# A four-layer graph network on one core: two single-head products in three rounded passes, one output slot, and another order of work in every queue

## What is computed

```
# x (128, 128, 512), adj (128, 128, 128); _ln = layer norm over the features
h = max(_ln(x), 0);  x = x + elu-attention, one head, values h           # layer 0
h = max(_ln(x), 0);  x = x + two GAT layers:                             # layer 1
      L1a: xl = h @ W1 (1024 columns, 4 heads), softmax over sources, elu
      L1b: xl2 = g @ W2 (512 columns, 1 head), softmax, out = attn^T @ xl2
h = max(_ln(x), 0);  x = x + attn(h) @ h, one head                       # layer 2
h = max(_ln(x), 0);  x = x + relu(attention, 8 heads of 64, h @ W_proj)  # layer 3
```

## Time and profile before

| | us |
|---|---|
| median of 3 runs | 3081.05 (3080.08 to 3081.91) |
| the profiled execution | 3083.84 |
| its span, first to last instruction | 3082.1 |
| TensorE busy | 2976.9 (97% of the span) |
| VectorE busy | 2480.0 (80%) |
| ScalarE busy | 2319.9 (75%) |
| GpSimd busy | 2263.2 (73%) |
| transfers: mean busy share of the 16 DMA engines | 35% |

### The profile page before, as it was taken

The page is one execution under the profiler, slowest core; times in us unless marked ns, Lnnn a source line. Parts: engine busy times, 40 slices in busy tenths (PEclk is TensorE's granted clock), DMA queues, the critical chain, the costliest instruction groups (busy, mean ns, idle before and its releaser), DMA issues. The chain is left out here.

```text
span 3082.1 us, 79166 instructions
## 1 busy us (share of the span) xinstructions
PE 2976.9 (97%) x21040; PEld 2746.1 (89%) x21040; DVE 2480.0 (80%) x8101; ACT 2319.9 (75%) x6433; POOL 2263.2 (73%) x3214
## 2 busy tenths in 40 slices
PE   7899999999999999999999999999999999999974
PEld 5789999999999999999999999999999999999964
DVE  3578888888888888888888888888888888888852
ACT  2567787778877788777787778877788777787752
POOL 3467777777777777777777777777777777777753
PEclk6999999999999999999999999999999999999985
DMA  5123333333333333333333333333333333333332
GB/s 195 34 69 123 117 119 122 108 124 118 119 123 106 125 117 119 122 109 122 118 119 121 108 122 120 120 118 112 121 120 119 118 110 122 120 120 119 96 107 93
DMA packets 205558, 355.71 MB, mean 115 GB/s; under 512 B 51904, under 2 KB 117568, under 8 KB 188736
## 3 DMA queue, kind: packets, MB, share of 16 engines
q1 hardware_dynamic: 205120, 350.66, 34.8%
HBM read 314.93 MB, written 35.59 MB: 114 GB/s over the span
## 5 line engine op out<-in xcount | busy, mean ns | idle before, releaser
L1454 POOL TENSOR_SCALAR rs<-mv,rs 128x1 f32<-128x1 f32 x512 | 357.6, 698 | 109.2 <-POOL rs L1451 108.8
L997 ACT ACTIVATE eT<-eT,tc 128x128 f32<-128x128 f32 x1024 | 314.1, 389 | 161.3 <-POOL eT L1534 161.3
L432 PE MATMUL bank_b<-w_hi,hT_hi 128*128 128x344 f32 x1536 | 419.8, 328 | 5.6 <-DVE g L1277 3.8
L432 PE MATMUL bank_c<-w_hi,g_hi 128*128 128x258 f32 x2048 | 414.1, 283 | 4.7 <-DVE x L1204 4.7
L432 PE MATMUL bank_c<-w_lo,g_hi 128*128 128x258 f32 x2048 | 414.5, 284 | 0.0
L432 PE MATMUL bank_b<-w_lo,hT_hi 128*128 128x344 f32 x1536 | 408.2, 320 | 0.0
L1329 DVE CUSTOM_DVE_ANT_0 t_all_L<-t_all_L,mask 128x128 f32<-128x128 f32 x1024 | 368.6, 413 | 27.0 <-DMA t_all_L<-t_dram_L 26.5
L432 PE MATMUL bank_b<-w_hi,hT_lo 128*128 128x344 f32 x1536 | 357.0, 327 | 0.0
L432 PE MATMUL bank_c<-w_hi,g_lo 128*128 128x258 f32 x2048 | 351.8, 284 | 0.0
L432 PE MATMUL bank_e<-w_hi,hT_hi 128*128 128x264 f32 x1024 | 341.1, 347 | 5.5 <-DVE out_sb L1372 5.4
L1540 POOL TENSOR_TENSOR eT<-eT,shift_all 128x512 f32<-128x512 f32 x256 | 331.1, 1294 | 4.6 <-ACT eT L997 4.4
(11 more groups left out here) (158 smaller groups left out, 8577.5 us busy)
## 6 DMA issues: line engine op xcount, KB each, us to landing
shift_all<-shift_dram SPq DMA_DIRECT2D x128, 1024.0 KB, 5.3
t_all_L<-t_dram_L SPq DMA_DIRECT2D x128, 512.0 KB, 3.7
x_in<-in_x SPq DMA_DIRECT2D x128, 256.0 KB, 2.6
t_all_L1a<-t_dram_L1a SPq DMA_DIRECT2D x128, 256.0 KB, 3.2
out<-out_sb SPq DMA_DIRECT2D x128, 256.0 KB, 3.1
t_all_L<-t_dram_L SPq DMA_DIRECT2D x256, 64.0 KB, 3.1
adj_in<-in_adj SPq DMA_DIRECT2D x128, 64.0 KB, 3.0
t_dram_L1a<-t_rows_L1a SPq DMA_DIRECT2D x512, 0.5 KB
```

Of the source, the lines that this page charges most:

```text
L432: last = mm(bank[:, 0:width], a[:, c * P:(c + 1) * P], w[:, c, b * width:(b + 1) * width], start=(first and c == chunks[0] and n == 0), st ...
L997: last = activation(eT[:, k, :], eT[:, k, :], ACT.Prelu, bias=tc3[:, k:k + 1], alpha=SLOPE)
L1454: ts(b, mv[layer][:, 0:1], r, -1.0, ALU.mult, ALU.mult).then_inc(sem(f"rs_made{layer}"), 1)
```

## The change

Two of the three single-head products, `product_L1b` and `product_L2`, are made like the projections, in three rounded passes (`product_of_parts`). They need four new parts each: the transposed probabilities are rounded as they leave PSUM (`pT_L1b`, `pT_L2`, now F32R), VectorE subtracts for their low part (`pT_lo_L1b`, `pT_lo_L2`), ScalarE rounds the values (`v_hi_L1b`, `v_hi_L2`), and VectorE (`v_lo_L1b`) or GpSimd (`v_lo_L2`) subtracts for theirs. The output tile has one slot where it had two, the probabilities are written over the scores (`p1 = e1`), and the scratch `product` has two rows where it had four, which makes `columns_L0` and `columns_L2` wait for each other. Two counters are folded into others (`bn_made` into `mv_made`, `ident_loaded` into `att_in`). The order of the calls is another one in all five queues, and where a step begins has moved: some calls that opened a step now close the one before, with the graph number one lower. On SyncE the small sends come ahead of the large spreads, and the store of the output and `spread_L2` close the step. SKEW is 11.

Left out below: the waits that only follow the renumbering.

```diff
-SKEW = 12
+SKEW = 11
...
-        XR, MR, LR, TR, X1R, X2R, X3R, OR = 3, 10, 8, 4, 3, 2, 4, 2
+        XR, MR, LR, TR, X1R, X2R, X3R, OR = 3, 10, 8, 4, 3, 2, 4, 1
...
-        product = sb("product", [P, 4, D], BF16)
+        product = sb("product", [P, 2, D], BF16)
...
-        p1 = {k: sb(f"p_{k}", [P, P]) for k in one}
-        pT1 = {k: sb(f"pT_{k}", [P, P]) for k in one}
+        p1 = e1
+        split = ("L1b", "L2")
+        pT1 = {k: sb(f"pT_{k}", [P, P], F32R if k in split else F32) for k in one}
+        pT1_lo = {k: sb(f"pT_lo_{k}", [P, P], F32R) for k in split}
+        v_hi = {k: sb(f"v_hi_{k}", [P, D], F32R) for k in split}
+        v_lo = {k: sb(f"v_lo_{k}", [P, D], F32R) for k in split}
...
-                dst = (x3[:, c, :] if c < 2 else out_sb[:, c - 2, :])
+                dst = (x3[:, c, :] if c < 2 else (out_sb[:, 0, :], xl2[:, 0:D])[c - 2])
...
                 load(t.graph(0))
-                store(t.graph(12))
-                spread_L2(t.graph(7))
                 send_L0(t.later_graph(2))
-                spread_L0(t.later_graph(2))
                 send_L1b(t.graph(5))
                 send_shift_L3(t.graph(10))
+                spread_L0(t.later_graph(2))
                 spread_L1b(t.graph(5))
                 spread_shift_L3(t.graph(10))
                 send_L1a(t.graph(3))
-                spread_L1a(t.graph(3))
                 send_L3(t.graph(9))
                 send_L2(t.graph(6))
+                spread_L1a(t.graph(3))
                 spread_L3(t.graph(9))
+                store(t.graph(11))
+                spread_L2(t.graph(6))
...
+            def product_of_parts(key, bank):
+                for n, (a, v) in enumerate(((pT1[key], v_hi[key]), (pT1[key], v_lo[key]), (pT1_lo[key], v_hi[key]))):
+                    last = mm(bank, a[:], v[:], start=(n == 0), stop=(n == 2))
+                last.then_inc(sem(f"{key}_out"), 1)
...
             def product_L2(t, g):
                 if g.live:
-                    pe.wait_ge(sem("L2_pT"), g.made())
-                    if t.full:
-                        pe.wait_ge(sem("L2_pT"), g.made())
...
+                        pe.wait_ge(sem("flat_copied"), g.made(2))
+                    product_of_parts("L2", bank_a[:])
...
             def product_L1b(t, g):
                 if g.live:
-                    pe.wait_ge(sem("L1b_pT"), g.made())
+                    pe.wait_ge(sem("L1b_pT_lo"), g.made())
+                    pe.wait_ge(sem("L1b_v_lo"), g.made())
...
-                    mm(bank_c[:, 1, :], pT1["L1b"][:], xl2[:, 0:D], start=True, stop=True).then_inc(sem("L1b_out"), 1)
+                    product_of_parts("L1b", bank_c[:, 1, :])
...
-                project_L1b_first_high(t, t.graph(5))
                 project_L1b_first_low(t, t.graph(5))
+                turn_h3(t, t.graph(9))
                 project_L1b_last(t, t.graph(5))
                 turn_mask(t, t.graph(3))
-                turn_h3(t, t.graph(9))
+                product_L3_last(t, t.graph(11))
                 turn_prob_L1a(t, t.graph(4))
-                product_L3_last(t, t.graph(11))
+                product_L3_first(t, t.graph(11))
+                turn_exp_L2(t, t.graph(7))
                 turn_h1(t, t.graph(3))
-                turn_mask_L3(t, t.graph(10))
                 product_L1a_last(t, t.graph(4))
                 product_L1a_first(t, t.graph(4))
-                product_L3_first(t, t.graph(11))
+                turn_mask_L3(t, t.graph(9))
                 project_L1a_last(t, t.graph(3))
-                turn_exp_L2(t, t.graph(7))
                 project_L3_last_high(t, t.graph(9))
+                project_L3_last_low(t, t.graph(9))
                 product_L2(t, t.graph(7))
-                project_L3_last_low(t, t.graph(9))
                 project_L1a_high(t, t.graph(3))
+                turn_exp_L0(t, t.later_graph(2))
                 turn_exp_L1b(t, t.graph(5))
-                turn_exp_L0(t, t.later_graph(2))
                 project_L1a_low(t, t.graph(3))
                 product_L1b(t, t.graph(5))
                 product_L0(t, t.later_graph(2))
                 project_L3_first(t, t.graph(9))
+                project_L1b_first_high(t, t.graph(4))
...
                 act.wait_ge(sem(f"{key}_max"), g.made())
-                act.wait_ge(sem(f"{key}_turned"), g.made(1))
                 act.wait_ge(sem(f"{key}_recip"), g.made(1))
...
+            def v_hi_L1b(g):
+                if g.live:
+                    act.wait_ge(sem("xl2_made"), g.made())
+                    act.wait_ge(sem("L1b_out"), g.made(1))
+                    activation(v_hi["L1b"][:], xl2[:, 0:D], ACT.Copy).then_inc(sem("L1b_v_hi"), 1)
+
+            def v_hi_L2(g):
+                if g.live:
+                    act.wait_ge(sem("h_made2"), g.made())
+                    act.wait_ge(sem("L2_out"), g.made(1))
+                    activation(v_hi["L2"][:], h[2][:], ACT.Copy).then_inc(sem("L2_v_hi"), 1)
...
-                leaky_L3_first(t.graph(11))
-                leaky_L1a(t.graph(4))
-                norm_0(t.later_graph(2))
                 exp_L1a(t.graph(4))
-                values_L3(t.graph(10))
-                exp_L3_last(t.graph(11))
                 norm_1(t.graph(3))
+                leaky_L2(t.graph(7))
+                hT_hi_L3(t.graph(9))
+                exp_L3_first(t.graph(11))
+                v_hi_L2(t.graph(7))
+                copy_mask(t.graph(3))
+                exp_L2(t.graph(7))
                 pT_L1a(t.graph(4))
-                copy_mask(t.graph(3))
-                hT_hi_L3(t.graph(9))
-                leaky_L2(t.graph(7))
+                pT_L2(t.graph(7))
                 hT_hi_L1a(t.graph(3))
-                exp_L3_first(t.graph(11))
+                norm_2(t.graph(6))
+                elu_last(t.graph(4))
+                v_hi_L1b(t.graph(5))
                 elu_first(t.graph(4))
-                exp_L2(t.graph(7))
-                copy_mask_L3(t.graph(10))
-                elu_last(t.graph(4))
-                pT_L2(t.graph(7))
                 leaky_L0(t.later_graph(2))
+                copy_mask_L3(t.graph(9))
                 g_hi_first(t.graph(4))
                 g_hi_last(t.graph(4))
+                leaky_L1b(t.graph(5))
                 exp_L0(t.later_graph(2))
-                leaky_L1b(t.graph(5))
-                norm_2(t.graph(6))
                 exp_L1b(t.graph(5))
-                pT_L1b(t.graph(5))
                 norm_3(t.graph(8))
                 pT_L0(t.later_graph(2))
+                pT_L1b(t.graph(5))
                 leaky_L3_last(t.graph(10))
+                leaky_L3_first(t.graph(10))
+                leaky_L1a(t.graph(3))
+                values_L3(t.graph(9))
+                norm_0(t.later_graph(1))
+                exp_L3_last(t.graph(10))
...
+            columns_issued = {0: 0, 2: 0}
+
             def score_columns(layer, g):
+                dve.wait_ge(sem(f"st_made{2 - layer}"), columns_issued[2 - layer])
+                columns_issued[layer] += 1
                 dve.wait_ge(sem(f"h_made{layer}"), g.made())
...
-                    last = nc.vector.tensor_tensor_reduce(product[:, layer + i, :], h[layer][:], row[layer][:], 1.0, first,
+                    last = nc.vector.tensor_tensor_reduce(product[:, i, :], h[layer][:], row[layer][:], 1.0, first,
...
+            def pT_lo_L1b(g):
+                if g.live:
+                    dve.wait_ge(sem("L1b_pT"), g.made())
+                    dve.wait_ge(sem("L1b_out"), g.made(1))
+                    tt(pT1_lo["L1b"][:], bank_c[:, 0, 0:P], pT1["L1b"][:].bitcast(F32), ALU.subtract).then_inc(sem("L1b_pT_lo"), 1)
+
+            def v_lo_L1b(g):
+                if g.live:
+                    dve.wait_ge(sem("L1b_v_hi"), g.made())
+                    dve.wait_ge(sem("L1b_out"), g.made(1))
+                    tt(v_lo["L1b"][:], xl2[:, 0:D], v_hi["L1b"][:].bitcast(F32), ALU.subtract).then_inc(sem("L1b_v_lo"), 1)
+
+            def pT_lo_L2(g):
+                if g.live:
+                    dve.wait_ge(sem("L2_pT"), g.made())
+                    dve.wait_ge(sem("L2_out"), g.made(1))
+                    tt(pT1_lo["L2"][:], bank_a[:, 0:P], pT1["L2"][:].bitcast(F32), ALU.subtract).then_inc(sem("L2_pT_lo"), 1)
...
-                residual_L0(t.later_graph(3))
-                stats_1(t.graph(3))
-                moments_3(t.graph(8))
+                sources_L3(t.graph(10))
                 moments_1(t.graph(3))
+                targets_L3(t.graph(10))
                 stats_2(t.graph(6))
                 most_L1a(t.graph(4))
+                most_L3_last(t.graph(10))
                 columns_L0(t.later_graph(2))
                 rows_L0(t.later_graph(2))
-                sources_L3(t.graph(10))
                 most_L3_first(t.graph(10))
-                targets_L3(t.graph(10))
                 recip_L1a(t.graph(4))
-                most_L3_last(t.graph(10))
-                rows_L1b(t.graph(5))
-                stats_0(t.later_graph(1))
```

(60 more changed lines are left out.)

56 lines of the change are left out of this document (34 added, 22 removed).

## The result

| | before | changed |
|---|---|---|
| median us (lowest to highest) | 3081.42 (3080.08 to 3081.91) | 3259.12 (3250.96 to 3259.44) |
| span of the profiled execution | 3082.1 | 3257.7 |
| first to last transpose of rows_L1b, by 127: the mean step | 22.58 | 24.05 |
| from that last transpose to the end | 114.7 | 104.7 |

The ratio is 1.0567, with a 95% interval of 1.0553 to 1.0580 (the kernel before has four runs here; 3081.05 was the median of three of them). The forecast was 3044, its range 3024 to 3074. 127 steps x 1.465 us are 186 us lost; the emptying gives 10 back, and the sum is the 176 us between the spans. So nearly everything happened in the steady step.

The account below looks back on a forecast made before the run. TensorE's queue was taken to set the 22.61 us step. 3083.8 - 43 (products) + 12 (chain A stalls) - 6 (emptying) - 2.8 (profiled execution to median) = 3044 us; range 3024 to 3074.

Parts of the forecast that it names:

- The products: product_L1b and product_L2 on TensorE: three rounded passes take 0.68 us against 0.86, saving 0.36 a step, 43 over the run.
- chain B: From the sends through spread_L0, GpSimd and VectorE to turn_exp_L0: 10.6 us against TensorE's 11.5, room some 0.7.
- the far bound of 0.43: Worst case for one rounded 512-column pass on TensorE: 0.43 us, making a product 1.29; chance 0.02.
- Sums per engine: Added work on ScalarE, GpSimd and VectorE makes none the bound; VectorE reaches 20.4 us, 92% of the new step.
- Chain A: Last probabilities, values_L1a through recip_L1a and prob_L1a to turn_prob_L1a: room 0 to 0.25 us, 0.1 a step booked.
- The port: GpSimd blocking VectorE's most_L3 reductions ahead of recip_L1a: 0 to 0.87 us lost a step, 0.25 taken.
- rival 2: A whole GpSimd instruction blocks one most_L3 reduction ahead of recip_L1a each step, 0.87 us; 3122 us, chance 0.11.
- Rival 1: Chain A or chain B becomes the bound, 0.3 us a step instead of 0.1; 3068, between 3058 and 3082; chance 0.18.
- Filling and emptying: Layer 3's last steps, 17.5 us each, get shorter with targets_L3 ahead of both halves of most_L3; 6 us in all.

Follow-up runs that it names:

- e1: Changed kernel's order, tiles and slots kept, but both products made as single full-precision ones; 3173.4 us.
- e2: Old kernel's order of work on every engine, with the three-pass products, shared probability tiles and one output slot; 3093.5 us.
- e13: e2 with targets_L3 moved ahead of most_L3_first and recip_L1a put between its reductions, behind the first two; 3072.3 us, 0.9971 of the kernel before.

## Why the prediction was wrong, point by point

The products were priced rightly. What failed is chain B: it was summed as an open path with 0.7 us of room, and it is part of a closed ring and took 1.7 us more than TensorE's way beside it (13.34 against 11.65). A second wait, for a bank, was in no term.

- **The products.** Right. Passes 0.23 apart, three in 0.70 (0.68 said); the far bound of 0.43 is out. The Trainium skill, page "TensorE: Matmul & The Clock Gate", section "Back-to-back issue gap", would give 0.216: the trace does not agree, 0.23.
- **Sums per engine.** Right that none becomes the bound by its sum: VectorE is busy 2032 of 2400 us. That said nothing on the time.
- **Chain A.** Nearly as forecast. The table shows almost nothing (TensorE waits for prob_L1a 10 times, 7.5 us in all), but by the starts the room is gone: prob_L1a ends at 1511.18 and turn_prob_L1a starts at 1511.24, and this distance has a median of 0.05 us in the steady steps, where it was 0.19 before. product_L3_last ahead of it takes 1.03 us to the next start instead of the 0.92 of e1, so the wait is about 0.1 a step, what was booked. The shown idle time leaves it out, since the modelled end of product_L3_last lies over it.
- **Chain B: the failed step.** It was written as a path with a start, "10.6 us from rows_L1b, which comes some 0.2 after project_L1b_last". TensorE's side was right: from the end of project_L1b_last (1510.15) to turn_exp_L0 (1523.49) it is 13.34 with the waits of 0.90 and 0.79 in it, 11.65 without, 11.5 said. The 0.2 was a guess and measured 1.38 (1511.53); the old trace has the row in VectorE's timeline, 1.10 behind the end of the group at 1516.19:

```profile
1517.29 0.20 DVE L1181 STREAM_TRANSPOSE t_rows_L1b<-bank_c 128x32 f32<-128x32 f32 x1
```

  rows_L1b is timed by VectorE's queue and not by TensorE. So the chain does not begin at TensorE at all; it closes, through turn_exp_L0, project_L1a_low and values_L1a, into VectorE's own queue, and has no room that TensorE could give it. Of 10.6 us, 11.96 were measured: masked_L0 to masked_L1b 3.87 instead of 3.04, since two small steps of scale_3 stood beside VectorE, one 0.32 us longer beside v_lo_L1b, which the change adds, and one 0.45 longer beside g_lo_first behind it; the sends with send_L1b 2.85 instead of 2.2 and signals. With the real start the room of 0.7 was a lack of 1.7 (11.65 less 13.34).
- **A wait that I did not name.** turn_h3 moved ahead fills bank_e, which product_L3_first needs; hT_lo_L3 has to read it first and lies behind rows_L1b on VectorE. TensorE's queue is moved, and I asked only what the moved groups wait for, not who waits for the bank they fill. 0.56 us a step.
- **The port.** In rival 2 it was placed at most_L3 ahead of recip_L1a. It hit at most_leaky_L3 (and at scale_3, above) instead, behind recip_L1a but ahead of rows_L1b, which the ring needs: 0.99 us for a 128x8 operation that took 0.17 before, ending (1511.20) with prob_L1a (1510.14 and 1.04). The price was about right (0.82 for 0.87), the place wrong, and "where nobody on TensorE waits" did not hold any more, since the new order has rows_L1b and its sends behind it.
- **Rival 1** had the right mechanism and a size of 0.3 us a step; it measured 1.8 against the forecast's 22.25. Its price was capped at the gain, 3082, for no reason that was given: a ring longer than TensorE's step costs all that it is longer.
- **Filling and emptying.** Direction right: 15.9 us a step instead of 17.5, 10 us in all against 6 said.

## To carry over

When a change moves the queues of several engines, follow each new chain back until it reaches something already on it: a path gets its room from TensorE, a ring gets none, and its length is the step. Ask of the chain's first instruction which queue times it, and read that row. And of the 0.28 us a step that the products save on TensorE in the old order, none shows in e2 and little in e13, the one kernel whose moved operation takes TensorE's wait away and misses both collisions of VectorE with GpSimd.
